# A three-layer graph network on one core: 22 of 25 states a pass multiplied in pairs with seven half products in place of eight

## The reference

```python
def _L0_gnn_ref(x, Ws_self, Ws_neigh, bs, src, dst):
    deg = segment_sum(ones_like(dst), dst, num_segments=n)
    inv_deg = (1.0 / clip(deg, 1.0))[:, None]
    h = x
    for l in range(3):
        neigh = segment_sum(h[src], dst, num_segments=n) * inv_deg
        h = h @ Ws_self[l] + neigh @ Ws_neigh[l] + bs[l]
        if l != 2:
            h = relu(h)
    return h

x = _layernorm(x + _L0_gnn_ref(x, ...))
x = _layernorm(x + _L1_gnn_ref(x, src, dst, edge_attr_20, edge_weight, edge_attr_4, ...))
```

## Time and profile before

| | |
|---|---|
| device time, median of 3 runs | 1944.8 us (1929.04 to 1958.04) |
| span of the profiled execution | 1942.4 us |
| PE busy | 1847.2 us (95%), 7910 instructions |
| DVE busy | 1175.3 us (61%), 1955 instructions |
| ACT busy | 623.7 us (32%), 1432 instructions |
| POOL busy | 1137.9 us (59%), 1087 instructions |

### The profile page before, as it was taken

How to read it: one execution, slowest core, us unless ns; L and a number is a source line. 1 busy time by engine, 2 the same in 40 slices (tenths; PEclk the granted TensorE clock), 3 DMA queues, 4 the chain that set the end, 5 groups by cost and what they waited for, 6 DMA issues and landing times.

```text
span 1942.4 us, 23120 instructions
## 1 busy us (share of the span) xinstructions
PE 1847.2 (95%) x7910; PEld 1133.5 (58%) x7910; DVE 1175.3 (61%) x1955; ACT 623.7 (32%) x1432; POOL 1137.9 (59%) x1087
## 2 busy tenths in 40 slices
PE   8999999999999989999999999999997699999987
PEld 4455555554555545555555556666665477777765
DVE  6866778677444433444344436555535489899977
ACT  1566532332000000000000000111115478788875
POOL 4400000364888877888788822777776667677770
PEclk9999999999999989999999999999998799999998
DMA  5365665433555344544444443566644234344340
GB/s 163 123 210 174 222 206 180 128 102 95 142 145 139 105 128 116 145 124 132 108 132 124 121 130 128 197 210 198 209 157 117 71 96 114 105 109 114 110 109 26
DMA packets 239540, 265.35 MB, mean 137 GB/s; under 512 B 130757, under 2 KB 176527, under 8 KB 239420
## 3 DMA queue, kind: packets, MB, share of 16 engines
q1 hardware_dynamic: 204028, 205.79, 34.7%
q0 software_dynamic: 34480, 57.58, 10.9%
q10 hardware_dynamic: 912, 0.46, 0.1%
HBM read 174.44 MB, written 89.27 MB: 136 GB/s over the span
## 4 chain that ended last, share of the span: by engine, by line
PE 70%; DVE 11%; issue 6%; ACT 4%; another core or an unknown queue 3%; POOL 3%; DMA 2%; SPq 0%; DVEq 0%; POOLq 0%; ACTq 0%
PE low L1228 37%; PE mid L1054 23%; PE low L1258 3%; PE top L1085 2%; DVE table L2023 1%; PE mid L1239 1%; ACT table L1491 1%; DVE sort L1831 1%; PE mid L1069 1%; DVE table L2026 1%; POOL sort L900 1%; POOL table L922 1%; DVE table L2040 1%; DVE wbuf L2002 1%
## 5 line engine op out<-in xcount | busy, mean ns | idle before, releaser
L1228 PE MATMUL low<-table,abuf 125*125 125x512 f16 x3750 | 844.0, 382 | 7.3 <-issue 7.2
L1228 PEld LDWEIGHTS low<-table,abuf 125*125 125x125 bf16 x3750 | 508.3, 137 | 315.2 <-issue 43.4
L1054 PE MATMUL mid<-wbuf,h_t 128*125 128x512 f32 x1200 | 556.5, 601 | 5.8 <-DVE st_out L1759 5.1
L917 POOL DMA_INDIRECT by_src<-scat_row,sort x416 | 487.1, 1171 | 126.1 <-issue 120.8
L922 POOL DMA_INDIRECT table<-msg_table,wbuf x270 | 294.3, 1090 | 128.3 <-issue 85.2
L1054 PEld LDWEIGHTS mid<-wbuf,h_t 128*125 128x125 f32 x1200 | 215.4, 189 | 217.3 <-issue 202.5
L1769 DVE SCALAR_TENSOR_TENSOR y<-low,inv_deg,st_in 125x512 f32<-125x512 f32 x75 | 56.1, 749 | 462.1 <-PE low L1228 309.7
L1713 DVE TENSOR_TENSOR abuf<-abuf,row_scale 125x750 bf16<-125x750 bf16 (+6 forms) x156 | 265.9, 1719 | 0.8
L949 POOL DMA_INDIRECT sort<-msg_table,sort x180 | 193.2, 1073 | 92.2 <-issue 54.5
L1258 PE MATMUL low<-table,wbuf 128*125 128x256 f32 x900 | 212.7, 387 | 18.1 <-ACT table L1491 11.2
L900 POOL TENSOR_TENSOR sort<-sort 128x416 f32<-128x416 f32 x26 | 31.9, 1226 | 320.7 <-DVE sort L1831 320.7
(11 more groups left out here) (245 smaller groups left out, 1595.8 us busy)
## 6 DMA issues: line engine op xcount, KB each, us to landing
abuf<-adj SPq DMA_DIRECT2D x75, 781.2 KB
adj<-table SPq DMA_DIRECT2D x25, 781.2 KB, 4.6
states<-st_out SPq DMA_DIRECT2D x75, 256.0 KB
st_in<-states SPq DMA_DIRECT2D x75, 256.0 KB
flips<-y_flip SPq DMA_DIRECT2D x48, 256.0 KB
h_t<-flips SPq DMA_DIRECT2D x192, 64.0 KB
early_rows<-sort POOLq DMA_DIRECT2D x35, 320.0 KB
table<-early_rows SPq DMA_DIRECT2D x24, 448.0 KB
```

The source lines that it names most:

```text
L917: pool.indirect_dma_start(out=by_src, out_offset=bass.IndirectOffsetOnAxis(ap=place_i[:, k * PIECE + j:k * PIECE + j + 1], axis=0), in_=sc ...
L1054: last = pe.matmul(to[0:TN, :], h_t[i % 2][:, k, 0:TN], weights[l % 2][:, a, k, :], start=k == 0, stop=k == KC - 1)
L1228: last = pe.matmul(p_agg[k % 2][0:TN, :], a_tile[k % 3][:, a, :], table[ps % 2][0:TN, a, h, :], start=a == 0 and h == 0, stop=a == TILES - ...
```

## The change

In the first two passes, states 0 to 21 of the next layer are no longer multiplied singly. Two states r and r + 1 form a pair. The four blocks of a pair (upper and lower half of `h_t`, each state) and the four of the weights (upper and lower half, `Wn` and `Ws`) make a 2 x 2 by 2 x 2 product, which Strassen's scheme (in Winograd's form) does with seven half products instead of eight. A half product is two matmuls of 128 x 512. A pair has 14 matmuls in place of 16; 11 pairs a pass, 22 in all. The layer's other three states a pass stay single.

Sums and differences are needed for that, and they go to DVE and ACT. `mix_weights` makes four half matrices once a layer, into the buffer of the weights that are not in use; so the third layer's weights are loaded at k == 25 in place of k == 2. `mix_states` makes three half states in `mixed` and one in place of a half of `h_t`. `copy_first` (ACT) and `unmix_first`, `unmix_rows` and `unmix_second` (DVE) put the results together from four PSUM banks (`p_pair`).

The order moves too. At an odd k from 3 to 23 (and 28 to 48) the pair r = k + 22, r + 1 begins, four half products at block 6 of the aggregate (`pair_first`), so r + 1 is the state that aggregate k - 2 has made; at k + 1 come the other three, at block 2 (`pair_second`). Rows of both states are made in round k + 1. `h_t` has four buffers (`HT`) in place of two. A single state that stays is multiplied at block 14. In the last rounds of a pass, the first scaling of the next adjacency moves behind the rows of the pair.

```diff
+HT = 4
+HALF = KC // 2
+PAIRED = 22
...
+    p_pair = [p_mid[:, b * D:(b + 1) * D] for b in range(4)]
...
+    def pair_begun(k):
+
+        r = k + PAIRED
+        return [r] if k < 2 * TILES and 3 <= k % TILES <= PAIRED + 1 and k % TILES % 2 else []
+
+    def pair_ended(k):
+        return pair_begun(k - 1) if k else []
...
-                if k == 2:
-                    sp.wait_ge(s_ps, TILES)
+                if k == TILES:
+                    sp.wait_ge(s_pn, TILES + PAIRED)
+                    sp.wait_ge(s_ps, TILES + PAIRED)
                     for a in range(2):
                         load_weights(2, a)
...
+            def pair_first(r):
+                q, l, n = r + 1, r // TILES, pair_number(r)
+                upper = weights[l % 2][:, 0, 0:HALF, :]
+                for i in (r, q):
+                    pe.wait_ge(s_fld[flips_to(i) % 2], flips_loaded(flips_to(i)))
+                pe.wait_ge(s_wmix, 1 + l)
+                pe.wait_ge(s_row, r)
+                pe.wait_ge(s_own, r)
+                pair_product(p_pair[0], h_t[q % HT][:, 0:HALF, :], upper).then_inc(s_half, 1)
+                pe.wait_ge(s_mixed, 1 + n + 1)
+                wm = weights[(l + 1) % 2]
+                pair_product(p_pair[1], mixed[:, 1, :, :], wm[:, 0, HALF:KC, :]).then_inc(s_half, 1)
+                pair_product(p_pair[2], mixed[:, 0, :, :], wm[:, 0, 0:HALF, :]).then_inc(s_half, 1)
+                pair_product(p_pair[3], h_t[r % HT][:, 0:HALF, :], wm[:, 1, 0:HALF, :]).then_inc(s_ps, 1)
+
+            def pair_second(r):
+                q, l = r + 1, r // TILES
+                w, wm = weights[l % 2], weights[(l + 1) % 2]
+                pe.wait_ge(s_own, r + 1)
+                pair_product(p_pair[3], h_t[r % HT][:, HALF:KC, :], wm[:, 1, HALF:KC, :], False).then_inc(s_pn, 1)
+                pair_product(p_pair[0], h_t[q % HT][:, HALF:KC, :], w[:, 0, HALF:KC, :], False).then_inc(s_pn, 1)
+                pair_product(p_pair[2], mixed[:, 2, :, :], w[:, 1, HALF:KC, :], False).then_inc(s_ps, 1)
...
+                    for r in pair_ended(k):
+                        if a == 2:
+                            pair_second(r)
+                    for r in pair_begun(k):
+                        if a == 6:
+                            pair_first(r)
...
+            def copy_first(r):
+
+                act.wait_ge(s_half, 1 + 4 * pair_number(r) + 1)
+                act.wait_ge(s_sto[(r + 1) % 2], loads_of(r - 1))
+                act.activation(st_out[(r + 1) % 2][0:TN, :], p_pair[0][0:TN, :], ACT.Copy).then_inc(s_half, 1)
...
+            def mix_weights(l):
...
+                ch.link(dve.tensor_tensor(to[:, 0, 0:HALF, :], w[:, 1, 0:HALF, :], w[:, 0, 0:HALF, :], ALU.subtract))
+                ch.link(dve.tensor_tensor(to[:, 0, HALF:KC, :], w[:, 1, HALF:KC, :], to[:, 0, 0:HALF, :], ALU.subtract))
+                dve.tensor_tensor(to[:, 1, 0:HALF, :], w[:, 1, HALF:KC, :], w[:, 1, 0:HALF, :], ALU.subtract)
+                dve.tensor_tensor(to[:, 1, HALF:KC, :], w[:, 0, HALF:KC, :], to[:, 0, HALF:KC, :], ALU.subtract).then_inc(s_wmix, 1)
+
+            def mix_states(r):
...
+                ch.link(dve.tensor_tensor(s1, upper_r, lower_r, ALU.add))
+                dve.tensor_tensor(upper_r, upper_q, upper_r, ALU.subtract)
+                ch.link(dve.tensor_tensor(s2, s1, upper_q, ALU.subtract))
+                dve.tensor_tensor(s4, lower_q, s2, ALU.subtract).then_inc(s_mixed, 1)
+
+            def unmix_first(r):
+                q, common = r + 1, st_out[(r + 1) % 2][0:TN, :]
+                dve.wait_ge(s_half, 1 + 4 * (pair_number(r) + 1))
+                ch.link(dve.tensor_tensor(common, common, p_pair[1][0:TN, :], ALU.add))
...
+                dve.tensor_tensor(p_pair[2][0:TN, :], p_pair[2][0:TN, :], bias[0:TN, r // TILES, :], ALU.add)
+                dve.wait_ge(s_ps, r + 1)
+                dve.wait_ge(s_sto[r % 2], loads_of(r - 2))
+                ch.link(dve.tensor_tensor(st_out[r % 2][0:TN, :], common, p_pair[3][0:TN, :], ALU.add))
+                dve.tensor_tensor(st_out[r % 2][0:TN, :], st_out[r % 2][0:TN, :], p_pair[2][0:TN, :], ALU.add).then_inc(s_own, 1)
...
                 if k and by_dma(i):
                     flip(i)
+                for one in pair_begun(k):
+                    mix_states(one)
...
-                if k + 1 < AGGS:
+                if k + 1 < AGGS and not pair_ended_last(k):
                     scale(k + 1, 0)
...
+                for one in pair_begun(k):
+                    unmix_first(one)
+                for one in pair_ended(k):
+                    unmix_rows(one)
+                    for i in (one, one + 1):
+                        row_scales(i)
+                        row_lo(i)
+                    unmix_second(one + 1)
+                if pair_ended_last(k):
+                    scale(k + 1, 0)
+                if k in (1, TILES + 1):
+                    mix_weights(k // TILES + 1)
```

More of the change, by code:

```diff
@@ L144, in gnn_kernel @@
     y_flip = sb("y_flip", [P, D])
-    h_t = [sb(f"h_t{b}", [P, KC, P]) for b in range(2)]
+    h_t = [sb(f"h_t{b}", [P, KC, P]) for b in range(HT)]
+    mixed = sb("mixed", [P, 3, KC // 2, TN])
+    deg_row = mixed[0:TILES, 0, 0, :]
     row_max = sb("row_max", [P, 1])
@@ L186, in gnn_kernel @@
     totals = sb("totals", [P, BINS])
-    start = sb("start", [P, BINS])
     base = sb("base", [P, BINS])
```

99 lines of the change are left out of this document (72 added, 27 removed).

## The result

The changed kernel takes 1991.2 us (median of 4 runs, 1978.3 to 2002.4) where the kernel before takes 1946.4 (4 runs, 1929.0 to 1958.0). The ratio is 1.0249, with a 95% interval of 1.0176 to 1.0322. One of its terms, that of pass two, had the wrong sign. The loss is clear of the noise; whether it is more than 2%, to which the prediction gave 0.45, the interval leaves open.

What follows compares the result with a forecast made beforehand. TensorE was taken to bound passes one and two, with VectorE's lag costing time in pass one after the change. 45.4 + 0.6 - 10.1 + 2 = +38 us takes the span from 1942.4 to 1980, median 1982; range 1942 to 2014.

Steps and rivals of the forecast that it cites:

- 44 matmuls less: Passes one and two: 22 pairs cost 14 matmuls in place of 16, removing 37.8 us of TensorE time.
- VectorE's rounds: Pass one, rounds 1 to 13: VectorE's rounds sum to 284.8 us, so the mean of aggregate 13 starts at 524.3.
- Stalls ahead of the mixed products of aggregates 3, 5, 9, 11 and 13, 6.6 to 9 us: Pass one: TensorE stands five times, 6.6 to 9 us each, until VectorE's mixing is done.
- where 3.0 was taken: Pass one, behind the five stalls: the lowered TensorE clock costs 3.0 us each, kept between 0 and 3.4.
- Pass two, -10.1: Pass two: 11 pairs save 18.9 us and lose 8.8 to waits for mixing, net -10.1.
- a mean wait of 0.8 us: TensorE's wait for mixing per pair after aggregate 14, averaged over 15 starts of the mean: 0.8 us.
- Weights and boundaries, +2: Third layer's weights loaded at aggregate 25, mixed at 26: +2 us, between -2 and +12.
- No PE gap beyond 1 us after aggregate 14: Sign for right: after aggregate 14, TensorE never idles more than 1 us.
- PE busy about 38 us less on half products: Sign for right: TensorE's busy time on half products falls by about 38 us.
- Neither sign for wrong: Signs against the forecast: mean of aggregate 13 before 500, or gaps over 2 us at most pairs of pass two.
- waits everywhere: Rival, chance 0.20: late means cost 2 us a pair and the weight load starves TensorE at aggregate 25; 2010 us.
- The rule that the prediction weighed against itself: TensorE's clock swings after frequent short idles: 16 short waits at 3 us each on top of 1982, giving 2030.

Runs made afterwards that it cites:

- the late pairs: Changed kernel with pairs of pass one only from aggregate 15 on, every pair begun at block 14 instead of 6: ratios 0.9789 and 0.9811 to the kernel before.
- the stage without a wait: Means 27 to 48 of the changed kernel with all 22 pairs, copy behind the second eviction, block 14 in pass two: 2023.3 us, ratio 1.0093.
- the first experiment: Changed kernel with pairs of pass one only from aggregate 15 on, weights mixed in round 14: 1936.8 us, ratio 0.9972 to the kernel before.
- More of VectorE's work: Changed kernel with the first mixing operation made four times more for six pairs of pass one, rounds 3 to 13: 2004.0 us in one execution.

## Why the prediction was right, and where it was wrong

- *44 matmuls less:* 88 records less, and 26.3 and 15.1 us gained in two executions by the 32 matmuls that the late pairs save (27.5 by their price). Right.
- *VectorE's rounds:* the forecast walked 13 rounds and came to 524.3; it is 516.2. No round is off by over 1.4 us. The largest share is in rounds 8 to 11, each 0.8 to 1.0 us shorter than the walk had them, and in round 13, 1.3 shorter. Undoing the pairs there gave back all of it, and more work there cost its full price: this part was the cause of the loss, as forecast.
- *Stalls ahead of the mixed products of aggregates 3, 5, 9, 11 and 13, 6.6 to 9 us:* they came at 8.2, 8.8, 5.8 and 6.3 in aggregates 5, 9, 11 and 13; in aggregate 3 only 2.8, since aggregate 2 had already lost 3.5 us to a wait for ScalarE's evictions that the forecast didn't have (row below). The clock fell behind them, as behind the stall of the earlier trace rows: 8 records took 5.3 to 6.7 us instead of 3.6, 1.7 to 3.1 lost where 3.0 was taken.
- *Pass two, -10.1:* this failed. The step was "a mean wait of 0.8 us", for 11 pairs 8.8 us lost. Against the stage without a wait (353.8) this execution lost 27 us where its pairs saved 17 (370.9 less 353.8). Two things were wrong. The wait itself: 20.0 us of idle time, 1.8 a pair. The forecast's 0.8 is over all 15 starts, but a mixing stands only behind every second of them (the means of 27, 29, ... 41), and over those eight the same sum gives 1.1; the rest is that the same means came later here. And the clock, for which the term had nothing: behind the three waits of some 4 us (aggregates 30, 40 and 44) 8 records took 5.3 us instead of 3.6, 5 us in all. (The last 2 of the 27 I have not traced.) The idle times of other executions with the same block 6 are 4.4, 10.8, 11.8 and 17.8 us, so 8.8 was inside what occurs, and far from this one.
- *Weights and boundaries, +2:* +3.1 in these two executions (-3.4 and +6.5), most of it matmuls that changed their stage (5.2 in the +6.5); in others the boundary of pass one alone takes 80 to 107 us, so that no run settles this term.
- *Sum:* 46 us without what the end of the span gave by chance, against 38. TensorE starts aggregate 14 at 516.0, 37 later than before where 45 was forecast; from there to the third layer it loses another 9 where 7.5 were to come back. So two misses, of 8 us and of 16, stand against each other in a sum that looks better than its parts, and that the profiled span of 1976.3 comes so near to 1980 is the chance of the last 11.9 us as well.
- *Its own signs:* of those for right, the copy that `unmix_first` of round 3 waits for came (10.0 us), and gaps of 6 us or more in three of the five aggregates. "No PE gap beyond 1 us after aggregate 14" did not: ten stand ahead of mixed products, two in pass one and eight in pass two. Nor did "PE busy about 38 us less on half products": the products' busy time fell from 556.5 to 543.2 (163.0, 137.0 and 243.2 for the single ones); of the 24 us that are missing some 16 are the lower clock behind the stalls (10.6 in pass one, 5 in pass two). Neither sign for wrong came, but the second was near: in pass two five of 11 pairs have gaps of over 2 us.
- *Rivals:* "waits everywhere", with its 2 us a pair, describes pass two of this execution better than the forecast does; its other half, TensorE starved at aggregate 25, did not show.
- *Small readings:* the line that gives 0.41 us for 250 elements gives 1.25 for 1024, not 1.22, and the 0.25 for a weight load stands in no row; neither moves the sum by 1 us.

The wait in aggregate 2, and then three kinds of wait ahead of mixed products, which show what a short wait does to the clock (timeline of TensorE in the changed kernel: start us, us, matmul records, [idle before]; then the windows behind two of them):

```profile
258.68 0.60 PE L1153 MATMUL top<-table 128*128 128x125 bf16 x4 [3.52 <-ACT table L1441]
...
329.54 5.74 PE L1102 MATMUL mid<-wbuf,mixed 128*125 128x512 f32 x8 [8.24 <-DVE mixed L1867]
...
415.44 5.46 PE L1102 MATMUL mid<-wbuf,mixed 128*125 128x512 f32 x8 [8.76 <-DVE mixed L1867]
...
811.79 5.26 PE L1102 MATMUL mid<-wbuf,mixed 128*125 128x512 f32 x8 [4.14 <-DVE mixed L1867]
...
849.28 3.70 PE L1102 MATMUL mid<-wbuf,mixed 128*125 128x512 f32 x8 [2.05 <-DVE mixed L1867]
...
917.89 3.60 PE L1102 MATMUL mid<-wbuf,mixed 128*125 128x512 f32 x8
```

```profile
811.80:817.00 5.20, 5.20 (x9) 2.33 (x10) 3.26 (x1) 0.60 (x1) 4.60 (x2) 0.70 0.55 181
...
849.30:853.00 3.70, 3.70 (x9) 1.77 (x10) 3.25 (x1) 0.60 (x1) 3.40 (x2) 1.00 0.65 226
```

In pass two a product behind a wait of 2.05 us takes 3.70 us, at the full clock, against 3.60 behind none; behind 4.14 us it takes 5.26, at 0.70. The rule that the prediction weighed against itself (the Trainium skill, "TensorE: Matmul & The Clock Gate", "A second HAM failure mode: psum-queue depth-cycling") says that short idle moments between groups of matmuls, if they come often enough, make the clock swing between its two levels; the prediction's rival priced each short wait by it. Here the trace does not agree for waits of up to 2.06 us, behind which the clock stayed at the higher level (2.4 GHz), and it does for those of 4 us and more. In all traces of the changed kernel and of the experiments, 39 waits of up to 2.06 us stand ahead of mixed products, and behind each of them 8 records took 3.70; behind each of 33 waits of 3.6 us and more they took over 5. In between it goes either way. Two rows of the first experiment, and one of the last (*More of VectorE's work*), each with its own wait:

```profile
914.73 5.31 PE L1103 MATMUL mid<-wbuf,mixed 128*125 128x512 f32 x8 [2.16 <-issue]
...
952.45 3.70 PE L1103 MATMUL mid<-wbuf,mixed 128*125 128x512 f32 x8 [2.23 <-DVE mixed L1868]
```

```profile
378.42 3.70 PE L1102 MATMUL mid<-wbuf,mixed 128*125 128x512 f32 x8 [3.38 <-DVE mixed L1869]
```

What stays open is why means start late in pass two. In the rows below (the timeline of all engines), SyncE and VectorE start at the same moment, and the two wait for one thing in common, TensorE's semaphore for the finished aggregate; but TensorE had gone through 12 matmuls of the next aggregate by 805.77.

```profile
805.77 1.88 PE L1102 MATMUL mid<-wbuf,h_t 128*125 128x512 f32 x4
...
808.03 0.35 SPq L687 DMA_DIRECT2D abuf<-adj  x1
808.04 0.75 DVE L1898 SCALAR_TENSOR_TENSOR y<-low,inv_deg,st_in 125x512 f32<-125x512 f32 x1 [8.32 <-remote]
```

GpSimd's loads are not the reason; no other was tried.

## What to carry to other kernels

Fewer operations on the engine that bounds the whole program were worth nothing here in a stage in which another engine sets the pace, and what was paid for them there was paid in full: read the bound by stage, and make such a change only where the engine that pays for it has time. Let what a late engine makes be used late: eight blocks' delay took a wait of up to 20 us from a pass, at no cost that the runs show. When a wait is taken from a stage's sum, take it from the instructions that will wait, not from all of their kind. And when a wait is opened, look at what stands behind it in the same queue, since it may only move there.
